# Attention values split into two arrays, the first feed-forward layer's operand moved, and other unread products at both ends

## The reference

```
mod = silu(c) @ wmod                        # per batch: sa, ca, ga, sb, cb, gb
h = layernorm(x) * (1 + ca) + sa
scores = (h * w_lhs) @ (h * w_rhs).T        # 1024 x 1024 per batch
x = x + ga * softmax(scores) @ h
h = layernorm(x) * (1 + cb) + sb
x = x + gb * (relu(h @ W1 + b1) @ W2 + b2)  # 256 -> 1024 -> 256
```

## Time and profile before

| | |
|---|---|
| median of 3 runs | 693.54 us (693.3 to 694.51) |
| span of the profiled execution, first to last instruction | 691.5 us |
| what lies around the span, by the median | 2.0 us |
| PE busy | 686.1 us, 99% of the span |
| PEld busy | 627.7 us, 91% |
| DVE, ACT, POOL busy | 558.4, 427.5, 361.7 us |
| DMA | 77.54 MB, mean 112 GB/s |

### The profile page before, as it was taken

One profiled execution on the slowest core, in us unless ns is written; L12 is line 12 of the kernel. 1 busy time (PEld: TensorE's weight loads), 2 busy tenths in 40 slices (PEclk: granted clock), 3 DMA queues, 4 the chain that ended last, 5 costly groups with the idle time before them and its releaser, 6 DMA issues.

```text
span 691.5 us, 13488 instructions
## 1 busy us (share of the span) xinstructions
PE 686.1 (99%) x4621; PEld 627.7 (91%) x4621; DVE 558.4 (81%) x1059; ACT 427.5 (62%) x625; POOL 361.7 (52%) x396
## 2 busy tenths in 40 slices
PE   9999999999999999999999999999999999999998
PEld 8688899998999989998999989999899998999997
DVE  5699989799898898978989799887989887876421
ACT  3265398736786367683786647864678634845562
POOL 3572576636654386352872458643665434523644
PEclk9999999999999999999999999999999999999999
DMA  8211761137431382315622266112843126003300
GB/s 294 81 49 59 204 193 55 39 107 252 123 100 56 103 232 91 99 61 179 180 67 90 67 226 185 61 38 98 258 121 99 46 91 221 1 1 100 100 31 30
DMA packets 61663, 77.54 MB, mean 112 GB/s; under 512 B 5632, under 2 KB 54336, under 8 KB 61632
## 3 DMA queue, kind: packets, MB, share of 16 engines
q1 hardware_dynamic: 61632, 77.14, 35.5%
HBM read 46.15 MB, written 30.97 MB: 112 GB/s over the span
## 4 chain that ended last, share of the span: by engine, by line
PE 94%; DVE 4%; issue 0%; ACT 0%; DMA 0%; DVEq 0%; ACTq 0%; SPq 0%
PE col L595 9%; PE col L594 9%; PE col L593 9%; PE acc L530 8%; PE acc L531 8%; PE acc L536 8%; PE score L694 8%; PE score L690 8%; PE score L691 8%; PE score L578 4%; PE score L579 4%; PE score L580 4%; PE score L576 2%; PE score L584 2%; PE score L499 1%; DVE S L879 1%
## 5 line engine op out<-in xcount | busy, mean ns | idle before, releaser
L1088 POOL TENSOR_TENSOR hid_lo<-hid,hid_hi 128x512 fp32r<-128x512 f32 x127 | 175.4, 1386 | 143.2 <-ACT hid_hi L719 142.8
L715 ACT ACTIVATE hid<-col,b1T 128x512 f32<-128x512 f32 x128 | 87.0, 679 | 140.3 <-PE col L595 126.1
L530 PE MATMUL acc<-W2hi,hid_hi 128*128 128x256 f32 x480 | 119.2, 282 | 0.0
L531 PE MATMUL acc<-W2lo,hid_hi 128*128 128x256 f32 x480 | 116.9, 278 | 0.0
L690 PE MATMUL score<-V,Phi 128*128 128x258 f32 x448 | 108.8, 281 | 0.0
L691 PE MATMUL score<-V,Phi 128*128 128x256 f32 x448 | 108.6, 281 | 0.0
L719 ACT ACTIVATE hid_hi<-hid 128x512 fp32r<-128x512 f32 x128 | 81.0, 633 | 37.6 <-PE acc L536 29.8
L593 PE MATMUL col<-h2hi,W1hi 128*128 128x512 f32 x256 | 102.4, 400 | 0.0
L595 PE MATMUL col<-h2hi,W1lo 128*128 128x512 f32 x256 | 101.0, 395 | 0.0
L594 PE MATMUL col<-h2lo,W1hi 128*128 128x512 f32 x256 | 100.6, 393 | 0.0
L530 PEld LDWEIGHTS acc<-W2hi,hid_hi 128*128 128x128 f32 x480 | 90.4, 188 | 2.1
(11 more groups left out here) (139 smaller groups left out, 1493.2 us busy)
## 6 DMA issues: line engine op xcount, KB each, us to landing
block_rows<-blocks SPq DMA_DIRECT2D x29, 512.0 KB, 2.9
blocks<-block_rows SPq DMA_DIRECT2D x116, 128.0 KB, 3.0
x_cur<-x SPq DMA_DIRECT2D x16, 512.0 KB, 3.9
ln_t<-x SPq DMA_DIRECT2D x14, 512.0 KB, 4.8
score_blocks<-stage SPq DMA_DIRECT2D x14, 512.0 KB, 4.2
lower<-score_blocks SPq DMA_DIRECT2D x56, 128.0 KB, 2.9
out<-x_mlp SPq DMA_DIRECT2D x8, 512.0 KB, 3.0
out<-x_mlp SPq DMA_DIRECT2D x15, 256.0 KB, 2.2
```

Source lines behind the costliest of these rows:

```text
L530: nc.tensor.matmul(o, hi, W2hi[:, it, :], start=(it == 0 and (apart or t % 2 == 0)), stop=False, skip_group_check=True)
L531: nc.tensor.matmul(o, hi, W2lo[:, it, :], start=False, stop=False, skip_group_check=True)
L715: nc.scalar.activation(hid[:, n % 2, :], col[n % 2][:], ACT.Relu, bias=b1T[:, n % FT:n % FT + 1]).then_inc(col_read, 1)
L1088: G.tensor_tensor(hid_lo[:, n % RING, :], hid[:, n % 2, :], hid_hi[:, n % RING, :].bitcast(F32), ALU.subtract).then_inc(hid_lo_done, 1)
```

## The change

Three things, in the order of the diff:

1. V becomes two arrays. Vhi has rows of 1280 bytes: the high half, ones and zeros, and unused bytes. Vlo has rows of 1024 bytes: the low half alone. Small statistics arrays stand between the two, which sets where Vlo begins. The same 24 matmuls per AV step read them, in the same order, with the same widths.
2. The arrays behind V are declared in another order and with another filler, so that h2hi and h2lo start at another distance from W1hi and W1lo.
3. The unread products differ. At the start there are 6 of the identity instead of 20, then 5 of float32r of 32 stationary columns and 5 of 128 stationary columns whose moving operand is read with a step of two elements, both on a part of h2hi that DVE sets to zero before (L831 of the changed kernel). At the very end, behind the last GT tile, stand 30 products of 256 columns into col[0].

What the first two do to the addresses is arithmetic on the declared sizes. The distance is the start of the moving row less the start of the stationary block, in bytes within a partition, modulo 512; t is the tile:

| product | before | after |
|---|---|---|
| low half of V against Phi | 32 t | 448 for every t |
| high half of V against Phi or Plo | 16 + 32 t | 0 for even t, 256 for odd t |
| h2hi, h2lo against W1hi, W1lo | 64 | 256 |
| Rhi, Rlo against Lhi, Llo | 0 | 0 |
| W2hi, W2lo against hid_hi, hid_lo | 448 | 448 |

(L690 reads the low half before and the high half after; L691 the other.) Phi, Plo, L, R, W1, W2 and S keep their addresses; hid_hi and hid_lo move by 2048 bytes.

```diff
-    VP = D + 4
+    VP = D + 64
...
-            V_first = V_unsplit[:, :, VP:VP + VW]
-        V = sb("V", [P, T, 2 * VP], F32R)
-
-        sb("behind_V", [P, 96])
+            V_first = V_unsplit[:, :, 0:VW]
+        Vhi = sb("Vhi", [P, T, VP], F32R)
+        stats, stats1 = sb("stats", [P, HT, 6]), sb("stats1", [P, HT, 6])
+        mv1, nm1, rs1 = sb("mv1", [P, T, 2]), sb("nm1", [P, T]), sb("rs1", [P, T])
+        mv2, nm2, rs2 = sb("mv2", [P, T, 2]), sb("nm2", [P, T]), sb("rs2", [P, T])
+        Vlo = sb("Vlo", [P, T, D], F32R)
...
+        mod_l = sb("mod_l", [P, 2 * DK])
+        hid_hi, hid_lo = sb("hid_hi", [P, RING, HR], F32R), sb("hid_lo", [P, RING, HR], F32R)
+        mod_r = sb("mod_r", [P, 2 * DK])
+        sb("before_h2", [P, 40])
+        h2hi, h2lo = sb("h2hi", [P, DK, ROWS], F32R), sb("h2lo", [P, DK, ROWS], F32R)
...
+            def keep_busy_split(moving, stationary, out, count):
+                for _ in range(count):
+                    nc.tensor.matmul(out, stationary, moving, start=True, stop=True)
...                                                             # behind GT
+                        for at in (64, 96, 112, 0, 16, 32):
+                            keep_busy_split(h2hi[:, 0, 0:D], W1hi[:, 0, at:at + P], col[0][:, 0:D], 5)
                     elif kind == "MA":
                         pe.wait_ge(pool_const, 2)
-                        keep_busy(20)
+                        keep_busy(6)
+                        pe.wait_ge(const_ready, 3)
+
+                        keep_busy_split(h2hi[:, 0, 0:HR], h2hi[:, 0, HR:HR + QP], col[0][0:QP, :], 5)
+                        by_two = "p (n s) -> p s n"
+                        keep_busy_split(h2hi[:, 0, 0:HR].rearrange(by_two, s=2), h2hi[:, 0, HR:HR + P], col[0][:], 5)
...
-                            nc.tensor.matmul(o, Phi[:, slot, t, :], V[:, t, 0:VW], start=(t == 0), stop=False)
-                            nc.tensor.matmul(o[:, 0:D], Phi[:, slot, t, :], V[:, t, VP:VP + D], start=False, stop=False)
+                            nc.tensor.matmul(o, Phi[:, slot, t, :], Vhi[:, t, 0:VW], start=(t == 0), stop=False)
+                            nc.tensor.matmul(o[:, 0:D], Phi[:, slot, t, :], Vlo[:, t, :], start=False, stop=False)
...
-                            last = nc.tensor.matmul(o, Plo[:, slot, t, :], V[:, t, VP:VP + VW], start=False, stop=(t == T - 1))
+                            last = nc.tensor.matmul(o, Plo[:, slot, t, :], Vhi[:, t, 0:VW], start=False, stop=(t == T - 1))
...
+            V_.memset(h2hi[:, 0, :].bitcast(F32), 0.0).then_inc(const_ready, 1)
...
-                        for half in range(2):
-                            V_.memset(V[:, :, half * VP + D:half * VP + D + 1].bitcast(F32), 1.0)
-                            V_.memset(V[:, :, half * VP + D + 1:half * VP + VW].bitcast(F32), 0.0)
+                        V_.memset(Vhi[:, :, D:D + 1].bitcast(F32), 1.0)
+                        V_.memset(Vhi[:, :, D + 1:VW].bitcast(F32), 0.0)
```

More of the change, by code:

```diff
@@ L268, in block_kernel @@
         Rhi, Rlo = sb("Rhi", [P, DK, ROWS], F32R), sb("Rlo", [P, DK, ROWS], F32R)
-        with nc.sbuf_tensor("V_unsplit", [P, T, 2 * VP], F32) as V_unsplit:
-            V_first = V_unsplit[:, :, VP:VP + VW]
-        V = sb("V", [P, T, 2 * VP], F32R)
-        sb("behind_V", [P, 96])
+        with nc.sbuf_tensor("V_unsplit", [P, T, VP], F32) as V_unsplit:
+            V_first = V_unsplit[:, :, 0:VW]
[4 more added lines that the diff above has]
+        Vlo = sb("Vlo", [P, T, D], F32R)
         x_cur = sb("x_cur", [P, T, D])
@@ L284, in block_kernel @@
         hid = sb("hid", [P, 2, HR])
-        hid_hi, hid_lo = sb("hid_hi", [P, RING, HR], F32R), sb("hid_lo", [P, RING, HR], F32R)
-        h2hi, h2lo = sb("h2hi", [P, DK, ROWS], F32R), sb("h2lo", [P, DK, ROWS], F32R)
-        stats, stats1 = sb("stats", [P, HT, 6]), sb("stats1", [P, HT, 6])
-        mv1, nm1, rs1 = sb("mv1", [P, T, 2]), sb("nm1", [P, T]), sb("rs1", [P, T])
-        mv2, nm2, rs2 = sb("mv2", [P, T, 2]), sb("nm2", [P, T]), sb("rs2", [P, T])
         var_eps, half_power = sb("var_eps", [P, HT]), sb("half_power", [P, HT])
@@ L292, in block_kernel @@
         inv_sum = sb("inv_sum", [P, 1])
-        mod_l, mod_r = sb("mod_l", [P, 2 * DK]), sb("mod_r", [P, 2 * DK])
+        mod_l = sb("mod_l", [P, 2 * DK])
[3 more added lines that the diff above has]
+        h2hi, h2lo = sb("h2hi", [P, DK, ROWS], F32R), sb("h2lo", [P, DK, ROWS], F32R)
         wmod_a = S[:, 7, :].rearrange("p (k n) -> p k n", k=DK)
@@ L787, in part @@
                         act.wait_ge(av_done, T * b)
-                        nc.scalar.activation(V[:, n * HT:(n + 1) * HT, VP:VP + D], ln_v[:], ACT.Copy).then_inc(v_hi, 1)
+                        nc.scalar.activation(Vhi[:, n * HT:(n + 1) * HT, 0:D], ln_v[:], ACT.Copy).then_inc(v_hi, 1)
                     elif kind == "EX":
@@ L979, in part @@
                         dve.wait_ge(v_hi, 2 * b + n - 1)
-                        V_.tensor_tensor(V[:, tiles, 0:D], ln_v[:], V[:, tiles, VP:VP + D].bitcast(F32), ALU.subtract).then_inc(v_done, 1)
+                        V_.tensor_tensor(Vlo[:, tiles, :], ln_v[:], Vhi[:, tiles, 0:D].bitcast(F32), ALU.subtract).then_inc(v_done, 1)
                     elif kind in ("BH", "B2"):
```

## The result

The changed kernel takes 697.72 us (median of 4 runs, 697.39 to 699.3), the kernel before 693.64 (4 runs, 693.3 to 694.51): ratio 1.006, 95% interval 1.0047 to 1.0072. It is slower by 4.1 us, a small difference, but one that lies clear of the noise. The forecast was 688.7, faster by 4.8; its range ended at 696.5. The time of rival 3 was 697.5.

The account below looks back on a forecast made before the run. PE was taken as the bound, by matmul count times distance between starts. AV -3.9, F -1.3, start +0.1, end +0.3 make -4.8 on 691.5: 686.7, plus 2.0 around the span, 688.7 us; range 684.5 to 696.5.

Parts of the forecast that it names:

- rival 3: AV and F steps: 256 is a bad distance, AV step 2.88 us, F 1.40, 697.5 us in all; chance 0.18.
- What bounds the kernel: Whole kernel: PE busy 686.1 of 691.5 us, so matmul count times distance between starts sets the end.
- The rule of the Trainium skill: PE's operand reads: independent ports for moving operand and weight load, PE never waits, so the layout is worth nothing.
- Part 1: AV steps with V in two arrays: 2.78 us instead of 2.85, times 56, 3.9 us won.
- Part 2, F: F steps with h2 moved to distance 256: 1.375 us instead of 1.385, times 128, 1.3 us won.
- The G and score steps keep their distances [...] I take nothing: G and score steps: no change counted; settling sooner or later after AV or F worth 1.3 us either way.
- Part 3, the start: New unread products before the modulation: it starts between 7.6 and 8.1 us instead of 7.86; 0.1 us lost.
- the upper of the two cases: Five start products with a step of two: rate halved, 8.1 us, against 6.9 if the step costs nothing.
- the 5.2 us at which products get quicker: Start of PE: clock goes to full at about 5.2 us, identity products from 0.21 to 0.11 us each.
- Part 3, the end: 30 unread products behind the last one read: PE finishes with the stores or later, 0 to 0.5 us lost, 0.3 taken.

Follow-up runs that it names:

- h2_only: Kernel before with 192 bytes more ahead of h2hi, so h2 stands where the changed kernel has it; 695.96 us against 694.13 beside it.
- v_only: Kernel before with the values in two arrays as in the changed kernel, h2 left at its distance; 696.66 us against 694.13 beside it.
- ends_only: Kernel before with only the changed kernel's unread products at both ends; 694.62 us against 694.13 beside it, ratio interval 0.9998 to 1.0017.
- micro1: No computation: PE alone multiplies zeros in blocks at chosen distances, other compute engines at rest; 256 columns take 116.4 to 120.3 ns a product.
- replay2: PE alone, on zeros, two loop turns per layout, two-array values read low half first with 258 columns; values at (16, 176): second turn 82.21 us.
- replay3: PE alone, on zeros, two loop turns per layout, high half first with 258 columns; values at (16, 176): second turn 81.80 us, before 82.21.
- v_16_176: Kernel before with V rows of 2304 bytes, high half at distance 16, low at 176, high read first; 690.86 us against 694.01, ratio 0.9961.

## Why the prediction was wrong, point by point

- **What bounds the kernel**: right. PE bound it before and after, nobody waits inside the batches, and all of the difference lies in the distance between PE's starts. That addresses decide this distance was right too: PE alone shows it. The rule of the Trainium skill ("SBUF — State Buffer", "Who interferes with whom") that was weighed there agrees with the runs about the other engines, which change nothing here: some 0.03 us between replay and kernel. The step from it to a layout that is worth nothing fails: with one width and the other engines at rest the layout alone moves a product of 256 columns between 116.4 and 120.3 ns. Whether the loads and the moving rows get into each other's way, as the prediction reads it, no run shows.
- **Part 1, the step that failed**: "Low half: the distance of G, so G's settled 0.1133". It took the time that G reaches as belonging to the distance. It belongs to the sequence. In a turn of the changed kernel's loop the low half, which has G's distance, costs 121.3 ns a product for the 113.3 that were assumed; the high half costs 118.3 on Phi and 120.5 on Plo, where 120.0 was assumed for even tiles and 114.5 for odd ones, two distances that are one modulo 256. The AV step is 2.88, not 2.78, which times 56 is the forecast's largest term with the wrong sign: +1.7 for -3.9. The earlier trace rows already showed it in small: G does not begin at 0.1133, it gets there.
- **Part 2, F**: right in sign and near in size, -1.0 for -1.3, but partly by luck. It won only behind AV (2.72 for two steps against 2.80); behind G it is 2.75 against 2.74. And moved by itself (h2_only) it won 0.4, while in v_only, where it wasn't moved, it won 0.5.
- **Part 2, "The G and score steps keep their distances [...] I take nothing"**: the second failed step. The scores did keep their time. G has two states, 113.3 and 117.9 ns, and a step that begins behind a settled F at 0 stays in the slow one. It cost 2.4 us, above the 1.3 that was given as its bound, since that bound came from two steps behind AV and none behind F. Of the 2.4, 1.8 stand before the end of the last AV step; 0.6 stand behind it, where ends_only pays 0.7 with the addresses of before.
- **Part 3, the start**: +0.8 in the profile for +0.1. The products with a step of two cost twice the plain ones, which was the upper of the two cases; with that, 8.1 us was given, and ends_only has 8.07. The step that failed is the 5.2 us at which products get quicker: it was read from one profile and taken as fixed, and it lies between 4.8 and 6.8. It makes 0.6 of the 0.8, and that part is not the change's by these rows. The prediction calls it a change of the clock; the rows list the granted clock as 1.00 throughout and show only the rate.
- **Part 3, the end**: +0.4 for +0.3, right; ends_only, which leaves the addresses alone, has +0.4 too.
- **Rival 3** had the time (697.5) for a reason that is mostly wrong. Its AV step of 2.88 is what was measured. But 256 is not a distance of its own, the low half pays more than the high one, and F did not go to 1.40. What it lacked in F, G paid. So the time is a coincidence. Its argument, that alternating between two offsets costs, is open: the same distances in blocks of eight make AV 22.86 for 23.04 in one order and 23.03 in the other.
- **The range** was too narrow above, because its upper end left half of rival 3 out and had no term for G.

The measured sum: +1.7 - 1.0 + 2.4 + 0.1 inside, less 0.2 in products not in the table, is 3.0 us; with +0.8 and +0.4 at the ends it is the 4.2 by which the span grew. Of these, 2.4 us stand in the seven batches, 0.36 in a turn of the loop, and the replay makes that difference on PE alone (0.42 a turn); the rest is the two ends and G's last stretch.

Not settled: what state it is that a product leaves to the next, what tips G in ends_only at equal addresses, and what sets the time at which the first products get quicker.

## What to carry to other kernels

When PE is bound by back-to-back products, a rate read from one step (G's 0.1133) can't be moved to another by matching one property, be it width or distance: price it as unknown between the fastest and slowest row, and give every neighbouring step that keeps its own addresses a term with both signs. Where such a layout is worth trying, replay PE's real sequence of widths and addresses alone on zeros; here it told the real turn to some 0.03 us in four layouts and chose one that wins 0.4%. Keep order and widths exact in it: with the other half first and the distances kept, that gain was gone. Judge a layout by all kinds of products together, since what AV wins, G can give back. And read the start of the program from more than one profile before a term of it goes into a sum.

## What the runs showed of the hardware that was not expected

- The distance from start to start of float32r products depends on the start of the moving row less the start of the stationary block modulo 256 bytes, with a spread at one width of 116.4 to 120.3 ns for 256 columns and 226.8 to 234.2 for 512 (micro1).
- It depends also on the products before: moving W2 and hid together by 128 bytes, with all distances kept, made a replayed turn 82.89 us instead of 82.38, and a G step at one distance runs at 113.3 to 118.3 ns a product by the distance of the F steps ahead of it (micro1).
- In the real loops each turn repeated the last to 1 ns from the second on (82.407, 82.407, 82.406 us in h2_only, after 82.440); ends_only shows that the state can still tip once, for 0.7 us, with no address changed.
- Which half of the values is read first, with the two extra columns, is worth 0.4 us a turn at equal distances (82.21 in replay2, 81.80 in replay3).
- A product of 512 columns whose moving operand is read with a step of two elements took 0.45 us where one without took 0.23 (ends_only).
- The same 40 identity products at the start took 6.1 us in one kernel (v_16_176) and 7.1 in another (v_only), since they went from 0.21 to 0.11 us each at 4.8 us in the one and 6.8 in the other; the modulation began at 7.61 and 8.60 us.
